# A cosformer, attention and expert kernel: shared PSUM banks, split fills, values in two stages per group, four transposes of maxima per group, and a new order of work

## What is computed

```python
xn = _layernorm(x)
x = x + cosformer(xn, ...) + moe(xn, ...)          # layer 0
xn = _layernorm(x)
x = x + causal_attention(xn, ...) + top1_moe(xn, ...)   # layer 1
```

## Time and profile before

| | |
|---|---|
| median of 3 runs | 1281.01 us (1279.68 to 1281.63) |
| the profiled execution, whole | 1282.22 us |
| its span, first to last instruction | 1281.0 us |
| TensorE busy, products | 1207.4 us, 94% |
| TensorE busy, weight loads | 701.2 us, 55% |
| VectorE, ScalarE, GpSimd busy | 905.3, 914.9, 645.1 us |
| mean granted TensorE clock | 0.97 of full |

### The profile page before, as it was taken

One profiled execution on the slowest core, in us unless ns is written; L12 is line 12 of the kernel. 1 busy time (PEld: TensorE's weight loads), 2 busy tenths in 40 slices (PEclk: granted clock), 3 DMA queues, 4 the chain that ended last, 5 costly groups with the idle time before them and its releaser, 6 DMA issues.

```text
span 1281.0 us, 28797 instructions
## 1 busy us (share of the span) xinstructions
PE 1207.4 (94%) x10217; PEld 701.2 (55%) x10217; DVE 905.3 (71%) x2434; ACT 914.9 (71%) x1233; POOL 645.1 (50%) x866
## 2 busy tenths in 40 slices
PE   5877999999999999999999999999997898889998
PEld 3334454545454545454554545454544376689998
DVE  5337888888887888888888888887868464345554
ACT  1243787878787878787877878787875667667775
POOL 3452646463646465555646464636363211148885
PEclk8888999999999999999999999999997699999999
DMA  7260516243342516060606052423427310035442
GB/s 244 66 130 21 110 32 141 59 82 82 58 95 46 115 29 131 14 130 11 129 22 119 25 115 57 84 76 64 95 45 207 83 56 16 14 46 62 59 59 26
DMA packets 93236, 97.89 MB, mean 76 GB/s; under 512 B 12840, under 2 KB 73000, under 8 KB 92712
## 3 DMA queue, kind: packets, MB, share of 16 engines
q1 hardware_dynamic: 80248, 86.41, 30.2%
q0 software_dynamic: 12416, 8.99, 5.6%
q10 hardware_dynamic: 432, 0.66, 0.1%
HBM read 69.12 MB, written 26.30 MB: 74 GB/s over the span
## 4 chain that ended last, share of the span: by engine, by line
PE 82%; DVE 6%; ACT 4%; issue 4%; POOL 3%; DMA 0%; ACTq 0%; SPq 0%; DVEq 0%; POOLq 0%
PE PS L636 11%; PE PS L673 10%; PE PS L472 10%; PE PS L520 10%; PE PS L602 6%; PE PS L621 6%; PE PS L684 5%; PE PS L453 4%; PE PS L611 2%; ACT flow L795 2%; PE PS L486 2%; PE PS L496 2%; PE PS L587 2%; PE PS L464 2%; POOL early L1216 1%
## 5 line engine op out<-in xcount | busy, mean ns | idle before, releaser
L1229 POOL TENSOR_SCALAR_AFFINE_SELECT flow<-flow 128x256 f32<-128x256 f32 (+1 forms) x448 | 192.2, 443 | 456.1 <-ACT flow L795 454.5
L795 ACT ACTIVATE flow<-PS 128x1024 f32<-128x1024 f32 x320 | 318.9, 1029 | 89.3 <-PE PS L621 88.7
L1053 DVE TENSOR_REDUCE nm<-PS 128x2 f32<-128x1024 f32 x128 | 153.7, 1220 | 64.6 <-PE PS L587 64.2
L636 PE MATMUL PS<-flow 128*32 128x512 f32 (+3 forms) x2048 | 183.5, 455 | 2.2 <-POOL flow L1229 1.3
L520 PE MATMUL PS<-early,down 128*128 128x512 f32 x288 | 156.3, 635 | 5.8 <-POOL early L1216 4.9
L1216 POOL TENSOR_TENSOR early<-early 128x512 f32<-128x512 f32 x128 | 158.3, 1265 | 4.9 <-DMA early<-gate_rows 4.6
L472 PE MATMUL PS<-xnT,up 128*128 128x512 f32 x288 | 150.2, 623 | 4.0 <-DVE at L972 3.7
L786 ACT COPY qp<-PS 2x1024 f16<-2x1024 f16 x128 | 128.4, 1003 | 26.8 <-PE PS L611 24.9
L673 PE MATMUL PS<-xsT,w1s 128*128 128x128 f32 x1152 | 141.6, 276 | 2.2 <-DVE act L1151 2.2
L1253 POOL DMA_INDIRECT out_y<-X,rowu x72 | 112.0, 1555 | 62.3 <-ACT X L839 46.6
L1055 DVE TENSOR_REDUCE nm<-PS 128x2 f32<-128x768 f32 x128 | 121.8, 951 | 25.6 <-PE PS L587 25.5
(11 more groups left out here) (168 smaller groups left out, 2102.0 us busy)
## 6 DMA issues: line engine op xcount, KB each, us to landing
early<-gate_rows SPq DMA_DIRECT2D x128, 256.0 KB, 5.4
qp<-relay_q SPq DMA_DIRECT2D x64, 128.0 KB
kp<-relay_k SPq DMA_DIRECT2D x64, 128.0 KB
xsb<-xs SPq DMA_DIRECT2D x72, 65.0 KB, 1.9
relay_k<-qkh SPq DMA_DIRECT2D x32, 128.0 KB, 2.3
out_y<-X SPq DMA_DIRECT2D x16, 256.0 KB, 2.4
early<-in_w SPq DMA_DIRECT2D x1, 4096.0 KB, 16.1
relay_q<-qkh SPq DMA_DIRECT2D x16, 128.0 KB, 2.3
```

What stands on the lines that cost most here:

```text
L636: ins = pe.matmul(m.PS[32 * j:32 * j + 32, m.PV, kt * P:], m.vst[b % 2][:, kt, 4 * g + j, :], m.pt[:, r, k * L + o:k * L + o + L - kt * P] ...
L795: act.activation(m.pt[:, n % RING, :], m.PS[:, i:i + 2, :].rearrange("p k c -> p (k c)"), ACT.Exp, scale=1.0 / SCALE).then_inc(s["exp"], 1)
L1053: dve.tensor_reduce(nm[:, 3, 2 * n:2 * n + 2], ps, AX_X, ALU.max, negate=True).then_inc(s["max"], 1)
L1229: ins = pool.affine_select(part, part, [[0, part.shape[1]], [1, P]], ALU.is_ge, nothing, base=0, channel_multiplier=-1)
```

## The change

- **Values** (VALUES, `valued`, the counts NV): two stages per group instead of three, slots 0 and 1, then 2, 3 and 4. The ring of exponentials has 6 places instead of 4.
- **Maxima turned** (`mparts`, `mrows`, the tile `mt`): both pairs x of heads lie in one 128 column tile, 32 columns apart, so four transposes do for a group; ScalarE copies 2 rows of 512 columns four times instead of 2 rows of 1024 twice.
- **Banks** (`banks`): single stages take the bank longest unused of 0, 1, 2, 3, 5, 6, 7, with a handicap for banks last used as a pair; maxima and scores take the longest unused of the pairs (0, 1), (2, 3), (5, 6). In the experts' part they keep (0, 1) and (2, 3). A pair waits for both of its banks.
- **Fills**: `mt` is filled at GpSimd's start, vst[0] ahead of the first gated product of batch 0, vst[1] after the last; v of batch 0 waits for the one, v of batch 1 for the other.
- VectorE's wait for the first constants, with two small operations, goes from behind its first stage to the first kvr.
- **Places**: all are new (up to tile 30 of the experts); among them w1 from -19.5 to -30.389.
- Three small tiles are placed elsewhere in SBUF.

```diff
-RING = 4
+RING = 6
-VALUES = {1: (0, 1), 3: (2, 3), 4: (4,)}
+VALUES = {1: (0, 1), 4: (2, 3, 4)}
+NV = len(VALUES)
 def valued(n):
-    return 3 * (n // SL) + (1, 1, 2, 2, 3)[n % SL]
+    return NV * (n // SL) + (1, 1, 2, 2, 2)[n % SL]
...
+PAIRS = ((0, 1), (2, 3), (5, 6))
+SPLIT = 3
+PAIRED = (0, NBETWEEN + NBETWEEN % 2)
...
     def take():
-        at = turns.pop(0)
-        if at == held:
-            turns.append(at)
-            at = turns.pop(0)
-        turns.append(at)
+        if turns:
+            return turns[0]
+        at = min((at for at in (0, 1, 2, 3, 5, 6, 7) if at != held),
+                 key=lambda at: age[at] + (SPLIT if at < 7 and whole[at] else 0))
+        for one in PAIRS:
+            if at in one:
+                whole[one[0]] = whole[one[1]] = False
+        touch(at)
         return at
+
+    def take_pair():
+        got = min((one for one in pairs if held not in one), key=lambda one: max(age[one[0]], age[one[1]]))
+        for at in got:
+            touch(at)
+            whole[at] = True
+        return got
...
-    m.mt = sb("mt", [P, 2, NT, 2, P], F16)
+    m.mt = sb("mt", [P, 2, NT, P], F16)
...
-        for x in range(2):
-            for t in range(NT):
-                ins = pe.transpose(ps[:, x * L + t * P:x * L + (t + 1) * P], m.mt[:, g % 2, t, x, :], m.identh[:, :])
+        for t in range(NT):
+            ins = pe.transpose(ps[:, t * P:(t + 1) * P], m.mt[:, g % 2, t, :], m.identh[:, :])
...
-        for k in range(2):
-            at = 64 * k + MROW
-            ins = act.copy(m.qp[b % 2][at:at + 2, 2 * g:2 * g + 2, :], ps[at:at + 2, :, :])
+        for x in range(2):
+            for k in range(2):
+                at, turned = 64 * k + MROW, 64 * k + 32 * x
+                ins = act.copy(m.qp[b % 2][at:at + 2, 2 * g + x, :], ps[turned:turned + 2, :])
...
-        if b == 0:
-            act.wait_ge(s["fills"], 3)
+        if b < 2:
+            act.wait_ge(s["fills"], 2 * b + 3)
...
     def kvr(b, t):
+        if b == 0 and t == 0:
+            dve.wait_ge(s["d_first"], 16 * 3)
...
-        if b == 0:
-            fill()
...
     def gated(b, c):
         n, first = divmod(c - 1, CHUNKS)
+        if b == 0 and c == 1:
+            fill(0)
...
+        if b == 0 and c == NC - 1:
+            fill(1)
...
+    pool.memset(m.mt[:, :, :, :], 0.0).then_inc(s["fills"], 1)
```

More of the change, by code:

```diff
@@ L125 @@
 FIRST = placed(
[L126 to L137, removed]
-SECOND = placed(
[L139 to L153, removed]
@@ L154 @@
-ATTENTION = placed(
[L155 to L166, removed]
@@ new lines @@
+    norm0=[-49.057],
+    xnT0=[-47.786],
+    kvr=[-46.922, -45.731, -45.728, -44.77],
+    up=[-42.665, -40.737, -38.785, -38.501, -38.442, -36.876, -36.66, -35.489, -34.449],
+    q=[-41.751],
+    kv=[-41.331],
+    route0=[-42.986],
+    gate=[-40.422],
+    attn0=[-40.173],
+    gT=[-39.945],
+    at0T=[-37.944])
+SECOND = placed(
+    down=[-34.855, -34.751, -33.817, -32.425, -31.899, -29.133, -29.051, -28.731, -28.704],
+    gated=[-37.556, -37.32, -36.942, -36.647, -36.101, -34.957, -32.339, -31.588],
+    x1=[-27.643],
+    stats1=[-27.25],
+    norm1=[-25.94],
+    xnT1=[-25.658],
+    rope=[-24.551, -22.979],
+    parts=[-24.018, -19.749],
+    relay=[-17.917],
+    v=[-19.073],
+    logits=[-22.589],
+    route1=[-20.324],
+    expert=[-19.589],
+    ranks=[-17.997],
+    sort=[-17.769, -17.734, -13.635, -9.004])
@@ new lines @@
+ATTENTION = placed(
+    score=[-0.564, 0.586, 1.58, 2.991, 5.933, 7.014, 8.967, 11.029, 12.082, 12.383, 13.463, 13.778, 14.269, 14.456,
+           14.546, 15.259, 15.756, 16.515, 16.659, 19.311],
+    max=[-9.041, -7.953, -6.62, -4.139, -2.021, -1.624, -1.614, 0.197, 0.722, 1.959, 3.077, 4.319, 4.552, 4.716,
+         5.126, 5.74, 6.973, 8.306, 9.706, 10.424],
+    mparts=[-1.774, 2.116, 7.241, 10.658],
+    mrows=[-1.374, 5.213, 10.556, 11.149],
+    value=[2.676, 9.758, 12.387, 14.034, 14.669, 16.226, 18.235, 20.306],
+    sums=[13.94, 20.393],
+    heads=[15.117, 21.524],
+    mT=[22.491],
+    out=[24.369],
+    store=[26.41])
@@ L245, in banks @@
         if name in ("max", "score"):
[L246 to L249 removed]
+            got = take_pair()
+            work[stage] = [(at, free[at]) for at in got]
+            for at in got:
+                free[at] = ("max", b * G * NU + i + 1) if name == "max" else ("exp", b * NS + i + 1)
         if name == "sums":
@@ L271, in banks @@
             at = 5 if i < NBETWEEN or i % 2 else 0
-            work[stage] = [(at, free[at])]
+            work[stage] = [(at, free[at]), (at + 1, free[at + 1])]
             free[at] = free[at + 1] = "glu", i + 1
@@ L408, in place @@
         m.slotu = sb("slotu", [P, NT], U32, side)
+    m.below = sb("below", [P, E1 + 1, E1])
+    m.mine = sb("mine", [P, 3, E1 + 1])
+    m.jc = sb("jc", [P, P])
     m.w2 = sb("w2", [P, E1 * FC * D])
@@ L568, in score_banks @@
     def score_banks(stage):
-        i, freed = work[stage][0]
-        if freed:
-            pe.wait_ge(s[freed[0]], freed[1])
+        for _, freed in work[stage]:
+            if freed:
+                pe.wait_ge(s[freed[0]], freed[1])
+        i = work[stage][0][0]
         return m.PS[:, i:i + 2, :]
@@ L669, in hidden @@
         pe.wait_ge(s["xsT"], n + 1)
-        bank(("hidden", 0, n))
+        for k in range(2 if n in PAIRED else 1):
+            bank(("hidden", 0, n), k)
         at = work[("hidden", 0, n)][0][0]
@@ L1158, in vector_program @@
     dve.wait_ge(s["d_x"], 16)
-    started = False
     for name, b, i in order:
@@ L1162, in vector_program @@
             share[name](b, i)
-            if not started:
-                started = True
-                dve.wait_ge(s["d_first"], 16 * 3)
-                dve.tensor_scalar(m.token[:, :], const(m, K_T), -float(L), None, ALU.add)
-                then(dve.tensor_copy(m.base[:, :], m.kc[:, int(KO[K_E]):int(KO[K_E]) + E1]))
 def pool_program(nc, m, s, order, work):
@@ L1194, in q, with fill @@
         pool.tensor_tensor(m.qs[:, 1, :], m.qT[:, :], const(m, K_COSB), ALU.mult).then_inc(s["qs"], 1)
[L1195 to L1208 removed]
+    def fill(i):
+        pool.memset(m.vst[i][:, :, :, :], 0.0).then_inc(s["fills"], 1)
+        pool.wait_ge(s["fills"], 2 * i + 2)
+        for half in range(2):
+            ones = m.vst[i][:, :, :, 16 * half + HD:16 * half + HD + 1].rearrange("p t (g j) d -> p t g j d", j=4)
+            for t in range(NT):
+                ins = pool.memset(ones[:, t, half::2, :, :], 1.0)
         ins.then_inc(s["fills"], 1)
```

70 lines of the change are left out of this document (30 added, 40 removed), and 54 rows, old and new, of tables (hidden, load, outputs, rows).

## The result

| | before | after |
|---|---|---|
| median, range | 1281.32 us (1279.68 to 1283.19, 4 runs) | 1240.07 us (1238.77 to 1240.42, 4 runs) |
| span of the profiled execution | 1281.0 us | 1238.6 us |
| ratio after / before, 95% | | 0.9679 [0.9656, 0.9702] |

A forecast was written before the change was run, and what follows sets the result against it. TensorE's work was taken to bound the kernel between 117 and 904 us. 1282.2 less head 5, steady 31.7 and tail 3.5 gave 1242.0, or 1240.8 us against the median; range 1231 to 1262 for 8 in 10.

The forecast's parts named there:

- TensorE bounds the steady batch: Between 117 and 904 us: the work given to TensorE sets the time, busy 60.34 of 60.50 us a batch.
- The second rival: Steady batches: TensorE is not the bound, 60.5 us a batch stays, only head and some tail gained; 1273 us, chance 0.06.
- Transposes 0.92 us: Steady batch on TensorE: four transposes fewer per group save 0.23 us a group, 0.92 us a batch.
- Crossings 1.8 us: Steady batch on TensorE: fewer changes between kinds of stage save 1.8 us a batch (1.5 to 2.2).
- New waits 0.3 us: Steady batch: waits opened by the new order, mainly around scores 8 to 18, cost 0.3 us a batch (0 to 1.5).
- The steady gain: Between 117 and 904 us: batches go from 60.54 to 58.1 us, 31.7 us gained over 13 batches.
- the first rival: Steady batches: waits for ScalarE's exponentials and copies give half back, 59.3 us a batch; 1257 us, chance 0.25.
- The merging of values: Steady batch on TensorE: 12 value stages become 8 with the same columns; nothing added beyond the crossings counted.
- Head 5 us: Up to 117 us: split fills no longer hold VectorE for 5.08 us; 5 us gained (3 to 6).
- The signs: In the head: VectorE's L924 at 0.2 us and TensorE's denominators (L496) starting near 20 us.
- Tail 3.5 us: Last batches, from 904 us: fewer crossings and transposes against longer copies; 3.5 us gained (2 lost to 8 gained).
- The distance behind the last output: From the last batch's output to the end, the experts' part: stays as it was.

The follow-up runs named there:

- a_t8: The changed kernel with eight transposes per group instead of four, the added four into columns nobody reads; 1251.51 us, ratio 0.9616 to the kernel before.
- b_t4: The kernel before with the four transposes (one mask tile, four copies of 512 columns) as the only part of the change; 1301.81 us, ratio 1.0004.
- a_cross: The changed kernel with six pairs of stages per batch exchanged in order, same instructions, twelve more crossings; 1313.38 us, ratio 1.009 to the kernel before.
- a_3v: The changed kernel with values in three stages a group again, ring of six kept; 1269.3 us, ratio 0.9898 to the kernel before.
- a_copy5: The changed kernel with one more 2 by 512 copy on ScalarE in each group; 1276.67 us, ratio 0.9957 to the kernel before.
- b_places: The kernel before with only the new places of all stages; 1403.02 us, ratio 1.0936.
- b_t4merge: The kernel before with four transposes, values of slots 2 to 4 merged and a ring of six; 1320.35 us, ratio 1.0159.
- a_head: The changed kernel with batch 0's query projection ahead of the first up product and its key relay ahead of batch 1's gate rows; 1241.55 us, ratio 0.9681.
- the first two sets: Kernel before with single parts or transposes plus merged values; then both kernels unchanged, and the changed kernel with more transposes or crossings; 1240 to 1320 us.

## Why the prediction was right, point by point

- **TensorE bounds the steady batch: right, and shown.** The second rival (60.5 us a batch, 1273) is out: q distances are 58.21 us, and a_t8 gives back 0.72 us for 0.9 us of TensorE work. The rule of the Trainium skill that was weighed (Perfetto Trace Analysis, Identifying the Most-Contended Engine) would have put TensorE at 51% by its weight loads (29.70 of 58.20), with room to spare. The page asks for the share of the peak arithmetic rate beside it, which was not worked out here. That a_t8 gets slower by nearly the whole of the added work contradicts the room.
- **Transposes 0.92 us: right.** Priced from the earlier trace rows at 0.23 a group, measured 0.22 for the same four.
- **Crossings 1.8 us: plausible, not shown alone.** Stage times priced as in the earlier trace rows sum to 57.65 us for the new order (an estimate), and the batch takes 58.21, so 60.54 - 0.92 - 57.65 = 1.97 us fell to crossings and merged value stages, against 1.8. A second estimate agrees. Added up from short distances between the same neighbours, seen in any of the 14 profiles, a batch's work is 59.0 us before, 58.1 in b_t4, 56.1 in the changed kernel and 57.9 in a_cross: 0.9 for the transposes, 2.0 for the rest, and 1.7 for the 12 crossings that a_cross adds. (Such sums lie below the real work, and may hold a wait where a pair of neighbours stands in one kernel alone; the differences are what counts.) The traces show the counts themselves: 24, 24 and 13 changes of kind a batch before, 18, 18 and 12 after. The experiment that was to measure them by themselves (a_cross) opened waits larger than its object.
- **New waits 0.3 us: 0.56 measured**, of which 0.24 at the place named in the forecast (values of slots 2 to 4 behind the last exponential). The row of the changed kernel, in the wait for a bank that follows them:

```profile
507.50 1.50 PE L663 MATMUL PS<-flow 128*32 128x384 f32 x24
509.20 0.40 PE L648 MATMUL PS<-qp,kp 34*128 34x384 f16 x4 [0.20 <-DVE nm L1089]
```

  The steady gain came to 30.9 us against 31.7. But this was the weakest term: it stood at 0.3 (0 to 1.5), and kernels next to this one have 2.8 (a_3v), 2.6 (a_copy5), 4.1 (a_cross) and 9.9 us (b_places) of waits a batch, all by the same estimate of work. The rows of the kernel before could not tell 0.56 from those; only sums of stage times over the new list, with each bank and ring place followed, could, and these had been made for the new list alone. That the first rival (ScalarE, 1257, chance 0.25) did not come is narrower than the sum made it look: one more 0.58 us copy a group costs 2.05 us a batch.
- **The merging of values as "nothing beyond the crossings counted": wrong as a part, without effect on the sum.** In the new order it is worth 2.0 us a batch (a_3v), by fewer stages that can wait; in the old order it costs 1.5 or more (b_t4merge against b_t4).
- **Head 5 us (3 to 6): 2.3 in the pair that was forecast, mis-sized and outside its own range.** The signs came in part: L957 takes its usual 0.23 us in all batches but 0 and 1 (0.77 to 0.93), and the denominators (L523) start sooner, though not near 20 us. In the changed kernel's head, VectorE and TensorE (against the earlier trace rows):

```profile
19.79 0.77 DVE L957 TENSOR_SCALAR kvm<-kc,PS 128x16 f32<-128x16 f32 x1
...
20.67 0.93 DVE L957 TENSOR_SCALAR kvm<-kc,PS 128x16 f32<-128x16 f32 x1
...
21.67 2.21 PE L523 MATMUL PS<-kvm,early 128*128 128x144 f32 x16 [1.27 <-DVE kvm L957]
```

  They start at 21.67 against 24.93, 3.3 us sooner and not 5: with up0 ahead of q, GpSimd's two products (from 19.44 and 20.49) meet L957. Then more of it was lost: x1 of batch 0 came 2.7 us sooner, of batch 1 0.9. The meeting isn't the whole reason, since a_head takes it away in batch 0 and gains nothing. Two things were missed. The hold of the fills varies with when VectorE's instruction comes. In the second profile of the kernel before L924 began at 18.21, beside GpSimd's second product (18.16 to 19.25), and took not 5.31 us but

```profile
18.21 2.81 DVE L924 TENSOR_SCALAR kvm<-kc,PS 128x16 f32<-128x16 f32 x1
...
19.39 1.64 DVE L924 TENSOR_SCALAR kvm<-kc,PS 128x16 f32<-128x16 f32 x1
```

  and the denominators started at 21.18. And q of batch 2 scatters by 2 to 3 us between profiles with the same head: 115.1 to 117.3 in five with the old places and fills, 113.8 with the fills alone, 113.6 to 117.0 in six with the new head (the changed kernel twice, a_t8, a_cross, a_3v, a_copy5). A head term of 5 was read from one profile; what it was worth, 2.3 us in the pair, is within that scatter.
- **Tail 3.5 us (2 lost to 8 gained): 9.2, just outside.** 7.8 us of it lie between q and out of the last batch (216.7 to 208.9 us, TensorE busy 192.1 and 184.3), 1.4 behind. The counted work was 5 us. The clock was at its low level for 6.8 + 30.7 us there before and for 6.8 + 17.1 + 3.4 + 3.4 after, 0.80 in place of 0.73 in the 70 us of the earlier trace rows; 6.8 us less at half speed are worth about 3.4, an estimate from those lengths. With the 5 of work that makes the sum, but the other kernels warn: 208.9 to 216.7 us among the seven profiles with the new order, 216.1 to 225.3 among the six with the old. The distance behind the last output, put at nothing, was 160.0 in the old and 158.6 in the new. It is 158.7 to 158.8 in the six other profiles of the new order and 159.8 to 160.0 in the five others of the old, so it is real; b_places, with the new places and nothing else of the change, has 158.6, so it comes with the new places. By which of them is open. "The change does not touch" the end was wrong by these 1.4 us.
- **The sum: part luck.** The two misses (-2.7 and +5.7) and the steady one (-0.8) leave 2.2 us of span; for the whole profiled execution 1242.0 was forecast and 1240.07 measured. Most of the gain (30.9 of 42.4 us) came the way that was forecast; that the total is this close is luck, as head and tail missed in opposite directions.

## What to carry to other kernels

Where a hand-written order keeps TensorE full, price its work from distances between starts, but treat the waits of the new order as the term that decides: here nearly the same work, in neighbouring orders, ran from 1240 to 1313 us, and the new places without the rest of the change took 1403. A part of such a change can hardly be valued alone: those tried in the old order, at its upper level, gave nothing clear of noise or cost time, and taking the merged values out of the new order cost 2.0 us a batch where the merging had been priced at nothing of its own. Before adding work to an engine that shows 83% busy, look at what is queued behind that work at the one place where another engine waits for it.

## What the runs showed of the hardware that was not expected

- One program had two levels of time, 1281 and 1300 us, on the same chip (by its number) at different times. Of the 19 us, 16 are a lag of 0.84 and 1.30 us between TensorE's modelled end and its readers' start, at one place of each batch, at a granted clock of 1.00. TensorE's semaphore updates are late only within 2 us of the start of an indirect DMA on GpSimd, 332 times in the eight profiles of the first two sets and never in the six others. Its cause is open.
- The same GpSimd work held the same VectorE operation for 5.31 us in one execution and for 2.81 in another (0.23 undisturbed): the three fills in the one (1.80 + 3.54), a product of 1.09 us and the first fill in the other (18.16 to 20.99), where VectorE got in ahead of the next fill. In the changed kernel one product, 1.09 us, made it 0.77 to 0.93. The Trainium skill (SBUF — State Buffer, Who interferes with whom) tells that of VectorE and GpSimd the first to issue gets the port pair that they share for its whole instruction, and the other is blocked. These rows agree, and show that VectorE may stand behind one, two or three instructions of GpSimd.
- Issuing the first leg of a relay 6.3 us sooner landed it 10.8 us sooner (75.4 in place of 86.2 us), and what waited for the second leg started no sooner: the second leg's last 128 KB copy was issued by 86.7 us and its reader began 7.9 us later, against 5.2 us in the changed kernel.
